# Sums of pair products in four column strips instead of two, and mixed weights built from long matmuls, transposes and an addition

## The reference

```python
x0 = x                       # [512, 39, 64]
h = x
for W in (W0, W1):           # W0 [39, 39, 128], W1 [39, 128, 128]
    h = jnp.einsum('bid,bjd,ijh->bhd', x0, h, W)
    outs.append(h)
out = jnp.concatenate(outs, axis=1).sum(axis=-1)     # [512, 256]
```

## Time and profile before

| | |
|---|---|
| median of 3 runs | 355.78 us (355.58 to 356.35) |
| profiled execution, whole | 357.09 us |
| its span | 355.3 us |
| TensorE busy | 341.1 us, 96% |
| weight loads busy | 321.8 us, 91% |
| DVE / ACT / POOL busy | 152.8 / 114.7 / 10.2 us |
| instructions | 11,893, of them 5,688 matmuls and 5,688 weight loads |
| setup until the first sums | 98.51 us |

### The profile page before, as it was taken

How to read it: one execution, slowest core, us unless ns; L and a number is a source line. 1 busy time by engine, 2 the same in 40 slices (tenths; PEclk the granted TensorE clock), 3 DMA queues, 4 the chain that set the end, 5 groups by cost and what they waited for, 6 DMA issues and landing times.

```text
span 355.3 us, 11893 instructions
## 1 busy us (share of the span) xinstructions
PE 341.1 (96%) x5688; PEld 321.8 (91%) x5688; DVE 152.8 (43%) x182; ACT 114.7 (32%) x210; POOL 10.2 (3%) x14
## 2 busy tenths in 40 slices
PE   0899999999998999999999999999999999999997
PEld 0566699999997999999999999999999999999996
DVE  3104559910039535808172680808177171903000
ACT  1266643333364052233205222421422141232300
POOL 9100000000000000000000000000000000000000
PEclk9999999999999999999999999999999999999999
DMA  8940334000022000820000063000006000000000
GB/s 307 383 96 2 136 161 148 2 1 2 2 57 96 2 4 4 199 100 4 17 2 4 2 160 141 2 18 2 4 3 145 9 2 17 4 2 4 4 0 15
DMA packets 4352, 20.06 MB, mean 56 GB/s; under 512 B 592, under 2 KB 1104, under 8 KB 3920
## 3 DMA queue, kind: packets, MB, share of 16 engines
q1 hardware_dynamic: 3728, 18.79, 16.3%
q10 hardware_dynamic: 576, 0.52, 0.4%
HBM read 18.78 MB, written 0.52 MB: 54 GB/s over the span
## 4 chain that ended last, share of the span: by engine, by line
PE 96%; DMA 1%; DVE 1%; issue 1%; SPq 0%; ACT 0%
PE out_ps L508 36%; PE stage L474 35%; PE stage L435 8%; PE stage L455 7%; PE stage L457 7%; PE stage L438 2%; DMA arena<-in_w_rows 1%; DVE arena L270 1%; DVE arena L272 0%; SPq L238 0%; ACT arena L399 0%
## 5 line engine op out<-in xcount | busy, mean ns | idle before, releaser
L508 PE MATMUL out_ps<-arena 114*128 114x128 f32 (+2 forms) x968 | 128.7, 294 | 0.0
L474 PE MATMUL stage<-arena 128*60 128x80 f32 (+4 forms) x4096 | 126.0, 227 | 1.6 <-issue 1.6
L474 PEld LDWEIGHTS stage<-arena 128*50 128x50 f32 (+2 forms) x4096 | 123.6, 128 | 3.7 <-issue 1.9
L508 PEld LDWEIGHTS out_ps<-arena 114*128 114x128 f32 (+1 forms) x968 | 121.7, 192 | 5.2
L408 ACT COPY arena<-stage 114x480 f32<-114x480 f32 (+4 forms) x136 | 72.5, 540 | 136.6 <-PE stage L474 136.6
L334 DVE TENSOR_TENSOR arena<-arena 128x3200 f32<-128x3200 f32 x16 | 55.8, 3487 | 59.6 <-PE stage L474 59.5
L435 PE MATMUL stage<-arena 128*128 128x380 f32 (+1 forms) x78 | 35.5, 539 | 10.0 <-DVE arena L272 10.0
L455 PE MATMUL stage<-arena 128*114 128x128 f32 x234 | 44.7, 273 | 0.0
L457 PE MATMUL stage<-arena 128*114 128x128 f32 x234 | 44.7, 273 | 0.0
L457 PEld LDWEIGHTS stage<-arena 128*114 128x114 f32 x234 | 33.6, 178 | 0.0
L455 PEld LDWEIGHTS stage<-arena 128*114 128x114 f32 x234 | 33.6, 178 | 0.0
(11 more groups left out here) (21 smaller groups left out, 35.1 us busy)
## 6 DMA issues: line engine op xcount, KB each, us to landing
arena<-in_x_dense SPq DMA_DIRECT2D x8, 640.0 KB, 6.4
arena<-in_x_single SPq DMA_DIRECT2D x16, 320.0 KB, 4.9
arena<-in_c_first SPq DMA_DIRECT2D x1, 2560.0 KB, 8.8
arena<-in_w SPq DMA_DIRECT2D x2, 640.0 KB, 6.8
arena<-in_c_second SPq DMA_DIRECT2D x1, 1280.0 KB, 5.2
arena<-in_w SPq DMA_DIRECT2D x1, 1216.0 KB, 9.5
arena<-in_w_square SPq DMA_DIRECT2D x1, 800.0 KB, 4.1
arena<-in_c_one SPq DMA_DIRECT2D x2, 256.0 KB, 9.8
```

The source lines that it names most:

```text
L474: done = nc.tensor.matmul(bank[PART * part:PART * part + r1 - r0, 0:count * 2 * some] .rearrange("p (i b) -> p b i", b=2 * some)[:, 2 * (t ...
L508: done = nc.tensor.matmul(to, sums, w, start=tile == 0 and s == 0, stop=last, skip_group_check=True)
```

## The change

The stationary columns of the sums are split at every 32 columns, so in four strips (32, 32, 32 and the rest) that write to adjoining partitions of the bank. The gaps vanish with this, and with them `place`, `PART`, `W_SPAN` and `X_SPAN`, and POOL's zeroing between parts. For the mixed weights each portion takes two banks: one for a single matmul of `w0_row0` by up to four fields of W1 (512 columns), one for up to four transposes of z. ACT copies the first bank to C, and DVE then adds the second bank to C. DVE adds the two half blocks between quarters in one instruction. Its order is cut up so that the additions come between other work. The sixteen passes are otherwise in the same order.

```diff
@@ constants
-PART = 64
-W_FIRST = 60
-X_FIRST = 50
-W_SPAN = PART + W_ROWS - W_FIRST
-X_SPAN = PART + X_ROWS - X_FIRST
+        STRIP = 32
+        PORTIONS = [(half, *portion) for half in range(2) for portion in weight_banks(half)]
+        SETUP_BANKS = FIELDS + 2 * len(PORTIONS)
+        def emptied_through(g):
+            return g - 2 * len(PORTIONS)
@@ gpsimd
-            def zero_between(h):
-                for at, rows in ((W_FIRST, PART - W_FIRST), (W_SPAN + X_FIRST, PART - X_FIRST)):
-                    nc.gpsimd.memset(view(z_other0[h] + at, (PAIR_SPAN, OTHERS[h]), (1, rows)), 0.0)\
-                        .then_inc(z_zeroed, 1)
...
-            pool.wait_ge(z_ready, 1)
-            zero_between(1)
@@ vector
+            def add_turned(k):
+                half, kind, i, n = PORTIONS[k]
+                c = c_place(half, kind, i, n)
+                rows = X_ROWS if kind == "x" else W_ROWS
+                bank = banks[(FIELDS + 2 * k + 1) % RING]
+                dve.wait_ge(filled, FIELDS + 2 * k + 2)
+                dve.wait_ge(c_copied, k + 1)
+                nc.vector.tensor_tensor(c, c, bank[0:rows, 0:n * HID].rearrange("p (s h) -> p s h", h=HID), ALU.add)\
+                    .then_inc(c_added, 1)
             dve.wait_ge(emptied, HALF)
-            mixed_weights(0)
+            mixed_of_quarters(0)
+            mixed_within_quarters(0)
             dve.wait_ge(emptied, FIELDS)
             dve.wait_ge(z_ready, 1)
-            mixed_weights(1)
+            mixed_of_quarters(1)
+            for k in range(5):
+                add_turned(k)
+            mixed_within_quarters(1)
             dve.wait_ge(z_ready, 2)
-            for u in range(UNITS):
+            for k in range(5, 20):
+                add_turned(k)
+            products(0)
+            for k in range(20, len(PORTIONS)):
+                add_turned(k)
+            for u in range(1, UNITS):
@@ scalar
+            for k, (half, kind, i, n) in enumerate(PORTIONS):
+                act.wait_ge(filled, g + (2 if half == 1 and kind != "x" else 1))
...
+                nc.scalar.copy(c_place(half, kind, i, n),
+                               banks[g % RING][0:rows, 0:n * HID].rearrange("p (s h) -> p s h", h=HID)).then_inc(c_copied, 1)
+                g += 2
@@ tensor
             def claim(g):
-                if g >= RING:
-                    pe.wait_ge(emptied, g - RING + 1)
+                last = g - RING
+                if last >= SETUP_BANKS:
+                    pe.wait_ge(emptied, emptied_through(last + 1))
+                elif last >= FIELDS:
+                    portion, turned = divmod(last - FIELDS, 2)
+                    pe.wait_ge(c_added if turned else c_copied, portion + 1)
+                elif last >= 0:
+                    pe.wait_ge(emptied, last + 1)
                 return banks[g % RING]
@@ mixed weights
+            for k, (half, kind, i, n) in enumerate(PORTIONS):
                 pe.wait_ge(z_ready, half + 1)
+                rows = X_ROWS if kind == "x" else W_ROWS
+                first = W_ROWS if kind == "x" else 0
+                nc.tensor.matmul(claim(g)[0:rows, 0:n * HID], view(w0_row0 + half * PAIR_ROWS + first, (1, rows)),
+                                 view(w1_0 + (first_field(half, kind) + i) * HID, (1, n * HID)),
+                                 start=True, stop=True).then_inc(filled, 1)
+                bank = claim(g + 1)
+                for m in range(i, i + n):
+                    z = z_own0[half] + m * W_ROWS if kind == "own" else z_other0[half] + m * PAIR_ROWS + first
+                    done = nc.tensor.transpose(bank[0:rows, (m - i) * HID:(m - i + 1) * HID], view(z, (1, rows)),
+                                               view(ident0, (1, HID)))
+                done.then_inc(filled, 1)
+                g += 2
@@ sums
-                for part, (r0, r1) in enumerate([(0, FIRST_PART[tile]), (FIRST_PART[tile], rows)]):
+                        for r0 in range(0, rows, STRIP):
+                            r1 = min(r0 + STRIP, rows)
+                            done = nc.tensor.matmul(
+                                bank[r0:r1, 0:count * 2 * some].rearrange("p (i b) -> p b i", b=2 * some)
+                                [:, 2 * (t - t0):2 * (t - t0) + 2, :],
+                                view(prod0[(2 * p + hf) % PRODS] + in_unit * W_ROWS + r0, (1, r1 - r0)),
+                                view(single0 + t * SLOTS + first, (PAIRS * SLOTS, 2), (1, count)), start=True, stop=True)
@@ order of passes
+            g = sum_pass(0, g)
+            for p in range(1, PASSES):
+                g = sum_pass(p, g)
+                weigh_pass(p - 1)
+            weigh_pass(PASSES - 1)
```

More of the change, by code:

```diff
@@ L182, in slot_of, with c_place @@
             return field if field < HALF else field + 1
-        SETUP_BANKS = FIELDS + sum(len(weight_banks(h)) for h in range(2))
+        PORTIONS = [(half, *portion) for half in range(2) for portion in weight_banks(half)]
+        SETUP_BANKS = FIELDS + 2 * len(PORTIONS)
+        def emptied_through(g):
+            return g - 2 * len(PORTIONS)
+        def c_place(half, kind, i, n):
+            if kind != "x":
+                return view(c_w0[half] + slot_of(first_field(half, kind) + i) * HID, (HID, n), (1, HID), rows=(0, W_ROWS))
+            if half == 0:
+                return view(c_xa0 + (1 + i) * HID, (HID, n), (1, HID), rows=(0, X_ROWS))
+            return view(c_xb0 + 2 * HID * i + HID, (2 * HID, n), (1, HID), rows=(0, X_ROWS))
         def banks_through(p):
@@ L302, in mixed_weights @@
                     step = EIGHTH * (width + n)
-                    add(view(zf + row, (10, 4), (1, k), (PAIR_SPAN, n)),
+                    add(view(zf + row, (10, 4), (1, k), (PAIR_ROWS, n)),
                         view(y + k * width, (step, 4), (n, k), (1, n)),
@@ L404, in _ @@
                 n, tile = divmod(p, TILES)
-                rows, count = SPAN[tile], COUNT[tile]
+                rows, count = ROWS[tile], COUNT[tile]
                 for t, some in groups(tile):
@@ new lines, in sum_pass @@
+            def sum_pass(p, g):
+                tile = p % TILES
+                rows, count, first = ROWS[tile], COUNT[tile], FIRST[tile]
+                for t0, some in groups(tile):
+                    bank = claim(g)
+                    for t in range(t0, t0 + some):
+                        hf, in_unit = divmod(t, HALF_PAIRS)
+                        if in_unit == 0:
+                            if tile == 0:
+                                pe.wait_ge(single_loaded[hf], 32 * (p // TILES + 1))
+                            pe.wait_ge(prod_ready, 2 * p + hf + 1)
+                        for r0 in range(0, rows, STRIP):
[5 more added lines that the diff above has]
+                                view(single0 + t * SLOTS + first, (PAIRS * SLOTS, 2), (1, count)), start=True, stop=True)
@@ L535 @@
     square[:, :fields, :fields] = w0.transpose(2, 0, 1)
-    rows, one = _np.zeros((2, hid, 2, W_SPAN + X_SPAN), f32), _np.zeros((2, 128, 4, hid), f32)
+    rows, one = _np.zeros((2, hid, 2, W_ROWS + X_ROWS), f32), _np.zeros((2, 128, 4, hid), f32)
     for half in range(2):
@@ L540 @@
                 continue
-            is_x = r >= W_ROWS
-            row = place(r - W_ROWS, X_FIRST) if is_x else place(r, W_FIRST)
-            tile, r = 2 * half + is_x, row + W_SPAN * is_x
+            tile, row = (2 * half, r) if r < W_ROWS else (2 * half + 1, r - W_ROWS)
             rows[0, :, half, r] = one[0, row, tile] = w0[f, g]
```

174 lines of the change are left out of this document (59 added, 115 removed).

## The result

The changed kernel takes 432.28 us (median of 4 runs, 430.52 to 433.85) against 355.89 before: ratio 1.2144, 95% interval 1.2089 to 1.2199. The profiled execution has a span of 429.6 us, 74.3 more than before. The forecast was 411 us in a range of 366 to 440.

What follows compares the result with a forecast made beforehand. TensorE's order of work bounds the kernel, and with four strips its instruction fetch: span 355.3 + 66.4 (fetch) - 1.64 (present stalls) - 9.6 (mixed weights) = 410.5, so 411 us measured, range 366 to 440.

Steps and rivals of the forecast that it cites:

- The mechanism: Passes of sums: four strips double the instructions, so TensorE waits for fetched blocks of 256; +66.4 us over four batches.
- T: Passes of sums: time of one fetch cycle per block of 256 instructions, 3.4 us, with bounds 3.06 and 3.73.
- What bounds it, and the array's prices: Sums: TensorE's work alone counts; four-strip rounds take 70.3 ns in tiles 0 and 2, 37.9 and 39.5 in tiles 1, 3.
- the rival of issue at 23.9 ns a record: Passes of sums: issue itself is the limit, a pass takes 12.2 us; +71 us, 416 us; chance 0.06.
- the rival of two at a time: Passes of sums: only two strips stream at once, tiles 0 and 2 take 18 us; +111, 455 us; chance 0.05.
- three full waits: Each pass of sums: the first of four blocks is there, the next three follow 3.4 us apart; 11.4 to 12.45 us.
- The third rival: Passes of sums: the fetch doesn't bind, the two earlier stalls came from loads beside them; 331 us; chance 0.13.
- the shorter cycle of 2.5 us: Passes of sums, rival: the fetch binds with a shorter cycle when no loads run; +23, 368 us; chance 0.08.
- near 101: Sign in the profile after: the first record of the weighings (L508 before the change) starts near 101 us.
- Mixed weights: Setup: long matmuls, transposes and additions by DVE let the stretch end at 88.9 instead of 98.51 us; 9.6 us gained.
- my two prices: Mixed weights: one fp32 transpose, if one record, costs between 97 and 109 ns; 97 was taken.
- The wait near 60 us: Mixed weights: TensorE, through portion 8 at 58.9, waits for DVE's addition 5 at 61.9; 3.0 us lost.

Runs made afterwards that it cites:

- experiment 3: Changed kernel without its fourth strip, rows from 96 on left out of sums and weighings: 371.94 us, ratio 1.041 to the kernel before.
- experiment 5: Changed kernel with 80 moving columns in tiles 1 and 3 too, all 40 slots streamed: 424.76 us, ratio 1.191 to the kernel before.
- experiment 4: Changed kernel with 40 instead of 80 moving columns in the sums of tiles 0 and 2: 441.51 us, ratio 1.241 to the kernel before.

## Why the prediction was right, and by how much it missed

The mechanism was right; that 432.28 lies in the range is in part luck. The forecast's own terms reached 427 at most (T at 3.73), and none of the rivals stands between that and 440: that part of the range had no term behind it. The terms below say what filled it.

**What bounds it, and the array's prices.** Right. When instructions are there, the first 175 records of the pass of tile 2 at 127.63 take 3.17 us, 18.1 ns each and 72 a round (70.3 forecast). The first 262 records of the pass of tile 3 at 145.36 take 2.84 us, 10.8 ns each and 43 a round (39.5 forecast). This refutes the rival of issue at 23.9 ns a record; four strips do stream side by side, which refutes the rival of two at a time. The floor of 25 ns in the Trainium skill ("TensorE: Matmul & The Clock Gate", Wait — 56ns, not 53.3ns?) doesn't hold across strips.

**The fetch.** The mechanism is right: 74 packets forecast and moved, pauses at every 128 records, tiles 1 and 3 at nearly the pace of tiles 0 and 2. T I took too small: 3.67 us against 3.4, of which 1.15 to the packet's start (1.15 forecast), 1.10 for the packet (1.03) and 1.43 until the engine goes on (1.2). The fourteen passes from 127.63 on have means of 12.86 us (tiles 0, 2) and 11.89 (tiles 1, 3), against 12.45 and 11.4 to 11.5: +6 us. But that isn't the price of the longer T. Three waits in each of fourteen passes would make it 42 x 0.27 = 11 us, and the lower clock in the last pieces of tiles 1 and 3, below, makes 6 more. About 11 came back, because a pass doesn't hold three full waits: the first pause of tiles 0 and 2 is 0.4 to 1.0 us, the later ones 0.95 to 1.6, and the passes at 145.36 and 187.91 have two pauses. So the count of three full waits was too high and T too low, and that the fetch comes out right for these passes is luck. The seen 3.73 us of the earlier trace rows, which I had set down as the end of the range, was nearer than the sum of the parts. The third rival, on the faster side, and the shorter cycle of 2.5 us fall with this: the shortest cycle is 3.37 us. The Trainium skill's statement that the refill is hidden ("Runtime: NRT & Kernel Launch", Instruction fetch mechanics) disagrees with these pauses; the measurement decides.

**The clock.** Not in the sum; I had only said what it would look like. L518 is busy for 137.9 us against 128.7, 9.2 us. Experiments 3 and 5, at a mean clock of 1.000 and 0.999, have the weighings at 129.3 and 129.2; experiment 4, at 0.844, at 150.3. To this come the last pieces of the seven passes of tiles 1 and 3: 746 records in 14.5 us at a clock of 0.50; at the full-clock pace of tile 1 (128 records in 1.40 us) they would take 8.2, so the clock cost 6.3 us there, by this estimate. So the clock cost some 15 of the 19 us: it is by far the largest part of the miss, and the term that the forecast lacked.

**Passes 0 and 1.** From the first sums to the first weighing it is 116.81 - 87.83 = 28.98 us, against 12.45 + 11.4 = 23.85 forecast, 5.1 more. The forecast took it that a weighing ahead of each pass gives the fetch time. Between passes 0 and 1 there is none: both passes of sums come before the first weighing, which therefore couldn't start "near 101" either. The trace shows the wait:

```profile
102.53 1.84 PE L485 MATMUL stage<-arena 128*32 128x40 f32 x128 [2.59 <-issue]
```

Pass 1 begins with a block and holds exactly four pieces of 128, so the weighing behind it waits for a block too: from 102.53 to 116.81 it is four cycles, 14.28 us, for three cycles and a block, 11.4. With the 2.59 us ahead of it that is 5.5; pass 0 itself took 12.1 us for 12.45, with 1.07 us of waiting for DVE's products(1) in it, which I had seen coming and priced at nothing ("about when the second half of pass 0 wants them"). The clock was down from about 103 us on (a mean of 0.51 from 102.9 to 120.0), but each block waited for its fetch, so it cost little here: experiment 5, at full clock, takes 28.70 us for the same stretch (88.76 to 117.46), with twice the columns in pass 1.

**Mixed weights.** -9.6 us forecast; the first sums start at 87.83 for 98.51, -10.7. A transpose is one record, and takes 0.44/4 = 0.11 us, the upper of my two prices, not 97 ns; the portion is 1.296 us:

```profile
61.27 0.86 PE stage L461 x2
62.13 0.44 PE stage L467 x4
```

What made up for it: DVE's addition takes 0.59 us in a row (2.95 us for five) instead of 0.69, and the whole of it began about 0.9 us earlier. The wait near 60 us is there. The sum is 6 + 9.2 + 5.1 - 1.1 = 19.2 us, against 429.6 - 410.5 = 19.1 of the spans; the first 6 are the low clock of the last pieces, by the estimate above.

## What to carry to other kernels

Count instructions as well as array time: where TensorE's program needs, in a long run of blocks, a new block of 256 instructions sooner than about 3.7 us after the last, splitting matmuls to load weights in parallel can make it slower, whatever the array gains. Two or three blocks in a row at 3.06 us passed without a pause, in the kernel before and in experiment 3. Look also at what stands between two such runs: other work with few instructions gives the fetch time, and where it is missing there is one wait more. Look for pauses exactly 128 records apart with nothing named in the chain; one pair of them in a kernel that is otherwise fine tells the price of doubling its instructions. Pauses cost twice, since the granted clock can fall behind them and make unchanged work longer; and evening out the demand by mixing two shapes on TensorE costs 0.34 us for each pair of changes.

## What the runs showed of the hardware that I had not expected

- Less array work can be slower: with half of the moving columns in half of the passes the kernel took 441.51 us for 432.28, and with twice the columns in the other half 424.76. The granted clock was 0.844, 0.917 and 0.999.
- Changing between column strips (of 64 here) and whole width costs about 0.34 us for the way there and back.
- Half of the columns at half of the clock take the same time: the last pieces of tiles 1 and 3 took 14.5 us in all with 40 or 42 moving columns at 0.50, and with 80 at 1.00.
- Four column strips stream fully side by side: a round of four records of 80 columns costs about what a round of two did (72 ns for 70.3), as long as instructions are there.
